# A graph network on one core: most of the next layer's rows are made inside a layer, and made again at its end

## The reference

```
for l in range(L):                                   # 3 layers
    X = jnp.einsum('ne,ref->rnf', out, weights[l])    # 9 relations
    msg = X[edge_type, src] + biases[l][edge_type]    # one row of 128 per edge
    hidden = jax.ops.segment_sum(msg, dest, num_segments=N)
    if l + 1 < L:
        hidden = jax.nn.relu(hidden)
    out = hidden
```

## Time and profile before

| | us |
|---|---|
| median of three executions | 4086.73 |
| the profiled execution | 4088.23 |
| its span, first to last instruction | 4086.4 |
| POOL busy | 2586.0 |
| DVE busy | 2730.2 |
| PE busy | 2874.2 |
| ACT busy | 820.6 |

### The profile page before, as it was taken

One profiled execution on the slowest core, in us unless ns is written; L12 is line 12 of the kernel. 1 busy time (PEld: TensorE's weight loads), 2 busy tenths in 40 slices (PEclk: granted clock), 3 DMA queues, 4 the chain that ended last, 5 costly groups with the idle time before them and its releaser, 6 DMA issues.

```text
span 4086.4 us, 56415 instructions
## 1 busy us (share of the span) xinstructions
PE 2874.2 (70%) x14077; PEld 1861.3 (46%) x14077; DVE 2730.2 (67%) x9147; ACT 820.6 (20%) x1995; POOL 2586.0 (63%) x2738
## 2 busy tenths in 40 slices
PE   7799966766677667666677666776775444446998
PEld 4455544444444444444444444444443333334776
DVE  9998875666666666666666566766664333337999
ACT  2588801001000100100100100000110000003665
POOL 0677757777777772777777777547777777771000
PEclk9899988888988898888888898888886555557999
DMA  4100013433332334342343333343333111113664
GB/s 157 50 2 2 2 43 77 84 75 73 86 78 73 83 82 161 82 83 73 78 84 75 73 86 78 98 153 76 72 85 80 53 53 53 53 53 103 189 191 141
DMA packets 373878, 336.39 MB, mean 82 GB/s; under 512 B 262034, under 2 KB 326090, under 8 KB 373448
## 3 DMA queue, kind: packets, MB, share of 16 engines
q0 software_dynamic: 87104, 158.80, 17.4%
q1 hardware_dynamic: 83112, 113.25, 8.3%
q10 hardware_dynamic: 203360, 60.73, 6.1%
HBM read 225.44 MB, written 107.13 MB: 81 GB/s over the span
## 4 chain that ended last, share of the span: by engine, by line
POOL 48%; PE 23%; issue 17%; DVE 9%; DMA 3%; ACT 1%; SPq 0%; DVEq 0%; POOLq 0%; ACTq 0%
POOL region L956 48%; PE ps L1033 9%; PE ps L1078 3%; DMA region<-x_of_type,arrays 3%; PE ps L1148 3%; PE ps L1118 2%; PE ps L1087 2%; PE ps L1176 2%; DVE region L399 1%; DVE region L738 1%; DVE region L626 1%; DVE arrays L433 1%; DVE arrays L444 1%; DVE region L560 1%; PE ps L1151 1%
## 5 line engine op out<-in xcount | busy, mean ns | idle before, releaser
L956 POOL DMA_INDIRECT region<-x_of_type,arrays x2418 | 2285.6, 945 | 902.8 <-issue 721.7
L1078 PE MATMUL ps<-region,oh 128*102 x5040 | 1146.8, 332 | 929.4 <-SPq L858 591.0
L1078 PEld LDWEIGHTS ps<-region,oh 128*102 128x102 f32 x5040 | 945.6, 210 | 1525.0 <-issue 1275.3
L555 DVE TENSOR_SCALAR oh<-iota_w,arrays 128x102 f32<-128x102 f32 x2528 | 727.2, 289 | 1253.7 <-PE ps L1078 1235.8
L1087 PE MATMUL ps<-region 128*128 128x510 f16 x4200 | 1411.1, 424 | 178.9 <-ACT ps L1234 132.9
L626 DVE TENSOR_TENSOR region<-region,ps 102x128 f32 x2520 | 714.5, 284 | 3.7 <-issue 3.5
L1087 PEld LDWEIGHTS ps<-region 128*128 128x128 f16 x4200 | 446.6, 107 | 253.7 <-issue 196.7
L1245 ACT COPY region<-ps 128x510 f32<-128x510 f32 x155 | 89.8, 579 | 2321.6 <-PE ps L1087 2321.1
L560 DVE TENSOR_SCALAR region<-ps,arrays 128x640 f16<-128x640 f16 x844 | 460.1, 545 | 0.0
L939 POOL DMA_INDIRECT scattered_edges<-region x304 | 296.2, 974 | 208.4 <-DVE shiftcol L463 110.6
L561 DVE TENSOR_SCALAR region<-ps,arrays 128x510 f16<-128x510 f16 x844 | 400.3, 474 | 0.0
(11 more groups left out here) (217 smaller groups left out, 1441.5 us busy)
## 6 DMA issues: line engine op xcount, KB each, us to landing
edge_counts<-region ACTq DMA_DIRECT2D x155, 255.0 KB
region<-x_of_type,arrays POOLq DMA_INDIRECT x2418, 2.5
arrays<-edge_counts SPq DMA_DIRECT2D x40, 960.0 KB, 5.1
x_of_type<-region SPq DMA_DIRECT2D x50, 576.0 KB, 2.8
edge_absent<-region ACTq DMA_DIRECT2D x155, 127.5 KB
region<-edge_absent SPq DMA_DIRECT2D x40, 480.0 KB, 4.2
x_of_type<-x0st SPq DMA_DIRECT2D x51, 192.0 KB, 1.9
scattered_edges<-region POOLq DMA_INDIRECT x304
```

The lines of the kernel that those rows point to most:

```text
L555: ins = nc_.tensor_scalar(oh[:, t % U, 0:RB], iota_r, rowf[:, t % NT:t % NT + 1], None, ALU.is_equal)
L956: pool.indirect_dma_start(out=grow[:, t % GR * D:(t % GR + 1) * D], out_offset=None, in_=xt, in_offset=bass.IndirectOffsetOnAxis(ap=gix[:, ...
L1078: mm = pe.matmul(ps[0:RB, 6 + n % 2, t * D:(t + 1) * D], oh[:, u % U, 0:RB], grow[:, bass.ds(at[u % PAIRS], D)], start=True, stop=True)
```

## The change

The next layer's rows of nodes whose groups are already summed are made inside the running layer. The 25 blocks are cut in five fifths of five blocks. The first four fifths need groups up to 6, 12, 18 and 25 (`REACH`); they are made in front of the turns 9, 16, 23 and 31 (`AT_TURN`), that is at the places 216, 384, 552 and 744, in the layers 0 and 1. Each time PE waits until all sums so far are added, transposes 7 or 6 groups, and makes 15 x through the two banks 6 and 7; SP stores the five blocks in the midst of its passing on, behind the tiles that begin 12 after that place, every second one.

At the end of a layer come first the last fifth (groups 25 to 30, blocks 20 to 24) and its stores, and then the groups 0 to 24 and the blocks 0 to 19 once more. The stores of this repeat carry a condition: they are skipped unless a flag is set, and the flag is set on the chip from the sorted edges if one of the four groups 6, 12, 18, 25 ends later than its place. A skipped store still counts on its semaphore. POOL waits for five stores in each buffer (four early ones and the late one) plus four more if the flag is set, with a value from a register. The rows of each layer have an HBM array of their own.

```diff
+    EARLY = NB // XU - 1
+    REACH = [P * XU * (k + 1) // RB + 1 if P * XU * (k + 1) % RB else P * XU * (k + 1) // RB for k in range(EARLY)]
+    GROUPS = [range(REACH[k - 1] if k else 0, REACH[k]) for k in range(EARLY)]
+    CUT = P * XU * EARLY // RB
+    LATE_GROUPS, AGAIN_GROUPS = range(CUT, MB), range(0, CUT)
+    AT_TURN = [-(-(REACH[k] * NT // MB + BODY) // BODY) for k in range(EARLY)]
+    PAIR_BANKS, ALL_BANKS = (6, 7), (5, 6, 7)
+    EARLY_STORES, ALL_STORES = EARLY + 1, 2 * EARLY + 1
+            STORE_AT[AT_TURN[k] * BODY + 12 + 2 * j] = b
...
+            for k in range(EARLY):
+                ins = nc_.tensor_scalar(overrun[:, k:k + 1], te[:, REACH[k] - 1:REACH[k]], float(AT_TURN[k] * BODY), None, ALU.is_gt)
+            step(ins)
+            step(nc_.tensor_reduce(overrun[:, EARLY:EARLY + 1], overrun[:, 0:EARLY], AX.X, ALU.max))
+            nc_.tensor_copy(again_made[:, 0:1], overrun[:, EARLY:EARLY + 1])
+            nc_.tensor_scalar(again_made[:, 1:2], overrun[:, EARLY:EARLY + 1], float(16 * EARLY), None, ALU.mult)
...
             for l in range(L):
                 if l:
-                    for n in range(HN):
-                        take_turned(l, n, True)
-                    for q in range(XQ):
-                        ...
+                    take_turned(LATE_GROUPS, ALL_BANKS)
+                    take_made(l, LATE_BLOCKS, ALL_BANKS)
+                    take_turned(AGAIN_GROUPS, ALL_BANKS)
+                    take_made(l, AGAIN_BLOCKS, ALL_BANKS, clear=True)
                     load_lanes(l)
...
+                for i in range(0, TURNS):
+                    if l < L - 1 and i in AT_TURN:
+                        k = AT_TURN.index(i)
+                        take_turned(GROUPS[k], PAIR_BANKS)
+                        take_made(l + 1, BLOCKS[k], PAIR_BANKS)
+                    take_tiles(l, i, i < full)
...
+            def store(l, b, cond=None):
+                given[0] += XC
+                sp.wait_ge(s_xe, given[0])
+                sp.dma_start(xv[l][b * P:(b + 1) * P, :, :],
+                             xst[:, b % XU, :].rearrange("p (r d) -> p r d", r=R), cond=cond).then_inc(s_xd[b % XU], 16)
             def pass_on(l):
                 for t in range(GT):
                     sp.wait_ge(s_g[t % GR], 16 * (ROUNDS * l + t // GR + 1))
                     sp.sem_inc(s_seq, 1)
+                    if l < L - 1 and t in STORE_AT:
+                        store(l + 1, STORE_AT[t])
...
             for l in range(1, L):
+                for b in LATE_BLOCKS:
+                    store(l, b)
+                for b in AGAIN_BLOCKS:
+                    store(l, b, needed)
                 pass_on(l)
...
             pool.wait_ge(s_d, marks["rows"])
+            again = values_of(pool, again_made, 1, 16 * EARLY, 1)[0]
...
                     for u in range(XU):
-                        pool.wait_ge(s_xd[u], 16 * XN * l)
+                        reg_wait(pool, s_xd[u], again + 16 * (ALL_STORES * (l - 1) + EARLY_STORES))
...
+            def turn_sums(groups, banks, added):
+                pe.wait_ge(s_add, added + 2 * SLOTS)
+                if made[0]:
+                    pe.wait_ge(s_xe, made[0])
...
+            def make_x(l, blocks, banks):
+                first = made[0]
+                for j, (b, c) in enumerate((b, c) for b in blocks for c in range(XC)):
+                    if j >= len(banks):
+                        pe.wait_ge(s_xe, first + j - len(banks) + 1)
...
             for l in range(L):
                 if l:
-                    turn_sums(l)
...
+                    turn_sums(LATE_GROUPS, ALL_BANKS, NT * l)
+                    make_x(l, LATE_BLOCKS, ALL_BANKS)
+                    turn_sums(AGAIN_GROUPS, ALL_BANKS, NT * l)
+                    make_x(l, AGAIN_BLOCKS, ALL_BANKS)
...
+                for i in range(0, TURNS):
+                    if l < L - 1 and i in AT_TURN:
+                        k = AT_TURN.index(i)
+                        turn_sums(GROUPS[k], PAIR_BANKS, NT * l + i * BODY)
+                        make_x(l + 1, BLOCKS[k], PAIR_BANKS)
+                        pe.wait_ge(s_xe, made[0])
+                    use_tiles(l, i, i < full)
```

More of the change, by code:

```diff
@@ new lines, in take_turned @@
+            def take_turned(groups, banks, relu=True):
+                for j, g in enumerate(range(groups[0], groups[-1] + 1, SLOTS)):
+                    lo, hi = g * RB, min(g + SLOTS, groups[-1] + 1) * RB
+                    dve.wait_ge(s_tn, turned[0] + 1)
+                    summed = ps[:, banks[j % len(banks)], 0:hi - lo]
+                    if relu:
+                        ins = nc_.tensor_scalar(hB[:, lo:hi], summed, 0.0, None, ALU.max)
+                    else:
+                        ins = nc_.tensor_copy(hB[:, lo:hi], summed)
+                    ins.then_inc(s_feat, 1)
+                    turned[0] += 1
@@ L658, in _ @@
-            for n in range(HN):
-                take_turned(L, n, False)
+                for i in range(0, TURNS):
[4 more added lines that the diff above has]
+                    take_tiles(l, i, i < full)
+            take_turned(range(MB), ALL_BANKS, relu=False)
             def moments(z, b):
@@ new lines, in turn_sums @@
+            def turn_sums(groups, banks, added):
+                pe.wait_ge(s_add, added + 2 * SLOTS)
+                if made[0]:
+                    pe.wait_ge(s_xe, made[0])
+                first = turned[0]
+                for j, lo in enumerate(range(groups[0], groups[-1] + 1, SLOTS)):
+                    if j >= len(banks):
+                        pe.wait_ge(s_feat, first + j - len(banks) + 1)
+                    for t, b in enumerate(range(lo, min(lo + SLOTS, groups[-1] + 1))):
+                        mm = pe.transpose(ps[:, banks[j % len(banks)], t * RB:(t + 1) * RB], hn[0:RB, b * D:(b + 1) * D],
@@ L1108, in turn_sums @@
                                           ident[0:RB, 0:RB])
                     mm.then_inc(s_tn, 1)
-                pe.wait_ge(s_feat, HN * l)
+                    turned[0] += 1
+                pe.wait_ge(s_feat, turned[0])
+            def make_x(l, blocks, banks):
+                first = made[0]
+                for j, (b, c) in enumerate((b, c) for b in blocks for c in range(XC)):
+                    if j >= len(banks):
+                        pe.wait_ge(s_xe, first + j - len(banks) + 1)
+                    pe.matmul(ps[:, banks[j % len(banks)], 0:G3], hB[:, b * P:(b + 1) * P],
+                              wsb[:, l * R + 3 * c:l * R + 3 * c + 3, :].rearrange("p r d -> p (r d)"),
+                              start=True, stop=True).then_inc(s_xm, 1)
+                    made[0] += 1
@@ L1127, in _ @@
-                if full < TURNS:
-                    for i in range(full, TURNS):
-                        use_tiles(l, i, False)
+                for i in range(0, TURNS):
[3 more added lines that the diff above has]
+                        make_x(l + 1, BLOCKS[k], PAIR_BANKS)
+                        pe.wait_ge(s_xe, made[0])
+                    use_tiles(l, i, i < full)
```

87 lines of the change are left out of this document (37 added, 50 removed).

## The result

The changed kernel takes 4011.37 us (median of four, 4011.01 to 4012.30); the kernel before took 4085.47 us in the same comparison. The ratio is 0.9813, 95% interval 0.9801 to 0.9826: 74 us less, where 67 were forecast (4020 us, range 4003 to 4062). Against the kernel before's own spread (4084 to 4089 us) and the changed kernel's (1.3 us) the difference is clear. The profiled execution took 4012.30 us, with a span of 4010.6 us against 4086.4 us: 75.8 us less.

The account below looks back on a forecast made before the run. POOL's gathers were taken to bound each layer, with PE and DVE following. The sum 82 - 10 - 3 - 2 = 67 us, against the profiled 4088.23 us and a median 1.5 us lower, gave 4020 us, range 4003 to 4062.

Parts of the forecast that it names:

- the ring: After each border, POOL stalls about 5 us at gather 60 until PE and DVE free places: -10 us, between 0 and -20.
- the last stretch: From place 744 to 840 PE needs 111 us, or 116, of 118 available: -3 us for both borders, 0 to -14.
- The bound: A layer lasts as long as its 806 gathers, 1007 us; moving POOL's first gather forward gains time one for one.
- The borders: POOL's first gather comes 40.5 us earlier at the first border and 41.5 us at the second, together 82 us.
- The pieces: Eight pieces inside the layers, 24 us each (21 to 29) of PE and DVE, hidden by POOL's lead of 42 us.
- Set-up: Before the first gather, flag instructions and waits cost 0.9 us and POOL's register load 1.1 us: -2 us (-1 to -3).
- The port lock: Rival: POOL's gathers slow beside DVE's x work, losing half to all of 84 us, 4063 to 4105 us; chance 0.06.
- Pieces not hidden, slower: Rival: POOL stands still during the eight pieces because its lead is near nothing; 125 us more, 4213 us; chance 0.05.

Follow-up runs that it names:

- e1: Changed kernel with the flag set always, so the repeat's stores are made and POOL waits for them: 4095.81 us, ratio 1.0018 to the kernel before.
- e2: Changed kernel without the repeat at a layer's end on PE, DVE and SP, flag still computed: 4006.29 us, ratio 0.9801 to the kernel before.
- e4: Changed kernel with each x matmul of the pieces inside the layers made three times: 4050.22 us, ratio 0.9906 to the kernel before.
- e3: Changed kernel with the last piece at turn 34 (place 816), not 31 (place 744): 4047.65 us, ratio 0.9898 to the kernel before.
- f1: The changed kernel again, unedited, on a slower chip: 5324.19 us, ratio 1.0269 to the kernel before there.

## Why the prediction was right

The mechanism was the one forecast: an earlier start of POOL at both borders, paid for at gather 60. The span gained 75.8 us where the sum said 67. The 9 us lie almost wholly in two terms that were put too high: the ring (10 counted, 3.0 measured) and the last stretch (3 counted, 0.7 measured, which is already in the 82.4 below).

- **The bound** (a layer lasts as long as its gathers, POOL's first gather counts one for one): shown by e1, which takes back the start and loses all, and by e2, which takes out 86 us of PE and DVE work and wins 5.
- **The borders, 82 us**: 82.4, and that close by luck. The first gather comes at 1575.74 and at 2613.85, 29.85 and 30.4 us behind the last one. The first border gave 71.3 - 28.9 = 42.4 us where 40.5 were counted: its 15 x took 12.5 us from 1559.10 and not 13.9, with the clock granted at 0.50 for the first 5 us of them and not for 8. The second gave 69.4 - 29.4 = 40.0 where 41.5 were counted: its 15 x took 11.6 us and not 10.4, and the turning came 0.7 us late. The two errors cancel; the mechanism, POOL waiting for 5 blocks instead of 25, is as foretold.
- **The ring, -10 us**: the place was right, gather 60, released by PE. The size was off: 2.1 and 0.9 us. PE's first place was at 1618.56 and not at 1619.5, and eight batches took 34 us from there (the last of their places at 1652.1), not 35.4; in the third layer PE's first place was at 2656.27, 42.4 us behind the first gather, and eight batches took 33 us. The end of a group's counts fell in them both times, as foretold. Small errors, but they all go one way and a stall is the difference of two long times.
- **The pieces, 24 us each, hidden by 42 us of lead**: 21 to 23 us without a place, no POOL wait; an x took 0.78 us through two banks, 0.85 forecast. The lead of 42 was measured in e4 as 41.5 and 40.8.
- **The last stretch, -3 us**: measured 0.0 and -0.7, so the term looks right, but its working was not. I counted 88 gathers left when PE reaches place 744, from the tile that the place reads. In the trace of the changed kernel PE's last matmul before the piece starts at 1441.8 and the last gather at 1545.9, which is 83 gathers; PE follows POOL by the landing and by a batch. So from there to the turning at 1557.26, less DVE's 3.3 us, PE had 112 us and not 118. It needed 22 us for the piece and 87 for the 24 batches, 109 to 110 where 111 was counted. Some 2 to 3 us were left and not 7, and 2.2 of them are the wait at 1540.09. e3 and e4 then cost 16 to 18 us a border where my count said 8 to 13.
- **Set-up, -2 us**: -2.2. From the start of POOL's load (536.1) to the first gather it is 1.7 us, of which the load is 0.50 where 1.1 was counted; the other 0.5 us lie ahead of it, where I had put 0.9 for the flag.
- **The port lock**: 35 gathers a border now run beside the bias adds and relu; the 33 that begin from 1575.7 to 1615.7 take 0.938 to 0.953 us, and the 1612 gathers of layers 1 and 2 have a mean of 0.945 us as before. No trace of it. The Trainium skill, SBUF — State Buffer, section Who interferes with whom, says that a DVE instruction with at most one SBUF input, outside the 2-port modes, does not contend with GpSimd. The trace agrees.
- **Pieces not hidden, slower**, the rival with 5% (its aside, "at half of it in hand it would be 4110", is a slip: 8 x 12 - 82 + 15 = 29 us more is 4117): it did not come in the comparison that was forecast, but something like it happens on the two other chips: 145 us slower in f1, and the eight waits behind the pieces are there. That I had priced 125 is no confirmation: that sum had 82 us won at the borders, and in f1 POOL still waits 80.3 and 78.5 us there. The point from which it decides was named as POOL's lead; in truth it was a speed, PE's and DVE's against POOL's, that I took for the same everywhere.

## What to carry to other kernels

Where one engine issues at its own pace and the others follow with room to spare, work may be doubled on the others for the sake of starting that engine earlier; the buffer's depth times the pace is what one interruption may cost, and the room per item is how fast it is made up. Count the room from where the follower is, not from what it reads: here the difference of 5 items, 6 us, was most of a margin of 7. And a kernel that spends its spare room is slower wherever that room is missing: the same change gave -1.9% in the comparison that was forecast and +2.7% on another chip.

## What the runs showed of the hardware

- A conditional DMA that is skipped costs SP 0.2 us of instructions (medians at the first border: 103 + 29 + 73 ns), moves no packets (83112 on its queue with and without them), still counts on its semaphore, and is counted as written bytes on the page.
- SP passes on a backlog of landed tiles at 0.07 us each (32 counts from 1616.1 to 1618.1). PE's first place at 1618.56 is put down to SP with 2.35 us, but PE's own two register loads, 1.07 us each, began at 1615.8 and 1616.9 and ran until 1618.0, so the backlog behind the repeat's stores cost PE half a microsecond at most.
- Two of the chips run the same kernel before in 5187 and 5179 us instead of 4088. In the profiles of the changed kernel there, PE pauses for microseconds between matmuls in some stretches, while the DVE adds (0.283 us) and POOL's gathers (0.947 us) keep their durations. At the borders the pauses are seen only while POOL gathers; the cause is open.
